# Attention scores on 32-row strips of TensorE, one strip for each head of a group of four, in place of a block-diagonal key matrix

## What is computed

```python
x = x + jnp.tanh(g_xattn[0]) * _L0_xattn_ref(_layernorm(x, axis=-1), ctx_1024, ctx_1024, mask_Bx1xS2_if1, ...)
x = x + jnp.tanh(g_ffn[0]) * _L0_ffn_ref(_layernorm(x, axis=-1), L0_ffn_W1, L0_ffn_b1, ...)
...
scores = jnp.einsum('bhqd,bhkd->bhqk', q, k) / math.sqrt(hd)
scores = jnp.where(m == 0, NEG_INF, scores)
p_attn = jax.nn.softmax(scores, axis=-1)
```

## Time and profile before

| what | us |
|---|---|
| median of three runs | 288.04 |
| the profiled execution | 287.01 |
| its span, first to last instruction | 285.2 |
| outside the span | 1.8 |

### The profile page before, as it was taken

One profiled execution on the slowest core, in us unless ns is written; L12 is line 12 of the kernel. 1 busy time (PEld: TensorE's weight loads), 2 busy tenths in 40 slices (PEclk: granted clock), 3 DMA queues, 4 the chain that ended last, 5 costly groups with the idle time before them and its releaser, 6 DMA issues.

```text
span 285.2 us, 11006 instructions
## 1 busy us (share of the span) xinstructions
PE 229.3 (80%) x3785; PEld 193.4 (68%) x3785; DVE 189.1 (66%) x639; ACT 164.9 (58%) x482; POOL 180.3 (63%) x222
## 2 busy tenths in 40 slices
PE   1357888987988987789879896598789899999950
PEld 1245677765866765667768675376689799999950
DVE  4546778788798888988867868886575344444310
ACT  1236669696677886568865886436464344444410
POOL 5366757568467889467896686704877654555550
PEclk9999999999799999979996999979999999999995
DMA  7801466546543673314351221333143443110100
GB/s 216 230 15 28 102 148 169 143 103 144 144 129 79 171 177 67 105 32 126 67 150 37 42 48 34 76 85 86 45 143 91 123 119 79 50 33 24 39 21 0
DMA packets 58537, 26.53 MB, mean 93 GB/s; under 512 B 38608, under 2 KB 53989, under 8 KB 58484
## 3 DMA queue, kind: packets, MB, share of 16 engines
q1 hardware_dynamic: 55204, 20.02, 29.3%
q0 software_dynamic: 2272, 4.46, 4.7%
q10 hardware_dynamic: 1008, 1.35, 1.6%
HBM read 16.57 MB, written 5.51 MB: 77 GB/s over the span
## 4 chain that ended last, share of the span: by engine, by line
PE 43%; DVE 19%; issue 11%; ACT 10%; POOL 5%; DMA 5%; SPq 3%; DVEq 0%; POOLq 0%
PE ps L752 13%; DVE mx L1240 5%; PE ps L771 4%; PE ps L795 4%; PE ps L770 3%; PE ps L733 3%; PE ps L735 3%; PE ps L734 3%; ACT vx L644 2%; DVE qk L1185 2%; SPq L411 2%; ACT kT L630 2%; DMA w_r<-in_W_last_row 2%; ACT qk L616 2%; DMA kbd<-kT 2%
## 5 line engine op out<-in xcount | busy, mean ns | idle before, releaser
L565 POOL DMA_INDIRECT out<-fin,got x39 | 37.9, 971 | 28.2 <-DVE fin L1299 23.4
L1240 DVE TENSOR_REDUCE mx<-ps 128x16 f16<-128x1024 f32 x32 | 39.0, 1219 | 12.8 <-PE ps L813 12.7
L752 PE MATMUL ps<-w_f,hT 128*128 x312 | 44.6, 286 | 0.1
L517 POOL DMA_INDIRECT rows<-x_all,dest_i x32 | 33.3, 1041 | 17.0 <-DVE x_all L1075 9.5
L795 PE MATMUL ps<-vx,pr 128*64 128x32 f32 x1024 | 38.0, 229 | 4.9 <-DVE on L1175 4.0
L795 PEld LDWEIGHTS ps<-vx,pr 128*64 128x64 f32 x1024 | 34.5, 144 | 8.9 <-issue 5.3
L544 POOL TENSOR_TENSOR rot<-qk,cf 128x256 f32<-128x256 f32 x32 | 23.4, 732 | 24.7 <-ACT qk L616 17.6
L752 PEld LDWEIGHTS ps<-w_f,hT 128*128 128x128 f32 x312 | 37.8, 191 | 1.1 <-issue 0.3
L1299 DVE SCALAR_TENSOR_TENSOR fin<-ps,got 128x128 f32<-128x128 f32 x39 | 13.7, 351 | 35.9 <-PE ps L752 35.9
L531 POOL TENSOR_TENSOR stk<-rot,stk 128x256 f16<-128x256 f32 x32 | 21.5, 671 | 20.4 <-DVE stk L1253 20.4
L594 ACT ACTIVATE pr<-ps 128x1024 f32<-128x1024 f32 x32 | 32.7, 1021 | 2.2 <-PE ps L843 1.6
(11 more groups left out here) (158 smaller groups left out, 585.1 us busy)
## 6 DMA issues: line engine op xcount, KB each, us to landing
kbd<-kT SPq DMA_DIRECT2D x128, 32.0 KB, 2.5
got<-rows SPq DMA_DIRECT2D x39, 72.0 KB, 2.0
w_f<-in_W_rows SPq DMA_DIRECT2D x8, 256.0 KB, 2.9
w_r<-in_W_last_row SPq DMA_DIRECT2D x8, 256.0 KB, 3.2
w_f<-in_L_ffn_W SPq DMA_DIRECT2D x8, 256.0 KB, 4.7
x_all<-in_x SPq DMA_DIRECT2D x3, 512.0 KB, 5.2
xt_all<-in_x_t SPq DMA_DIRECT2D x3, 512.0 KB, 4.8
ct_all<-in_ctx SPq DMA_DIRECT2D x3, 512.0 KB, 4.5
```

What stands on the lines that cost most here:

```text
L517: pool.indirect_dma_start(out=rows, out_offset=bass.IndirectOffsetOnAxis(ap=dest_i[:, t:t + 1], axis=0), in_=x_all[:, t, :], in_offset=Non ...
L565: pool.indirect_dma_start(out=out_d, out_offset=bass.IndirectOffsetOnAxis(ap=got_i[:, u % GOT, R_ID:R_ID + 1], axis=0), in_=fin[:, u % FRI ...
L752: mm = pe.matmul(o, hT[:, par, c, :], w2_f[:, bass.ds(e, 1), c, :].rearrange("p o n -> p (o n)"), start=False, stop=(c == FC - 1))
L1240: dve.tensor_reduce(mx[:, t % 2, :].rearrange("p (w h) -> p w h", w=2)[:, :, 0:8], ps_s[:, :].rearrange("p (w h k) -> p w h k", w=2, k=S), ...
```

## The change

`kbd`, its zeroing (L488 on POOL, L886 on DVE), its four semaphores and its 128 transfers go. `kT` becomes a ring of four tiles, and ACT waits ahead of L630 for the transposed scores of four tiles earlier where it waited for `kbd` transfers. The score products contract one 32-row strip: 32 products of 64 columns for a tile, in two halves of 16, the first at the old place, the second behind the transpose L825, with a wait for the first half's completion. The transposed scores take 16 selector products and 32 others, each on one strip and 64 output rows. DVE's maximum reads the same 1024 columns and writes 4 by 4 values where it wrote 2 by 8. SP sends its later loads without the step loop.

```diff
+            def scores(t, half):
+                s = t % RING
+                for a in range(NA):
+                    for b in range(2):
+                        for w in (half, half + 2):
+                            r, c = head_rows(w), (NA * w + a) * S
+                            mm = pe.matmul(ps_s[S * b:S * b + S, c:c + S], qT[r, s, a, S * b:S * b + S],
+                                           kT[r, s, a, S * b:S * b + S], start=True, stop=True)
+                return mm
...
-                    pe.wait_ge(kbd_ld[s], (t // RING) * 64 + 64)
+                    pe.wait_ge(kT_ev, t + 1)
                     pe.wait_ge(qT_ev, t + 1)
                     wait(pe, mx_done, t)
-                    for a in range(NA):
...
-                    mm.then_inc(s_done, 1)
+                    scores(t, 0).then_inc(half_done, 1)
...
                     pe.transpose(ps_onT, on[:, t % 2, :], ident).then_inc(onT_done, 1)
+                t = i - 2
+                if live(t):
+                    pe.wait_ge(half_done, t + 1)
+                    scores(t, 1).then_inc(s_done, 1)
...
                     for a in range(NA):
-                        for w in range(2):
-                            r, c = rows_half(w), (NA * w + a) * P
-                            pe.matmul(ps_st[:, c:c + P], sel_h[r, a, :], mxT[r, par, :], start=True, stop=False)
+                        for w in range(4):
+                            r, c, k = head_rows(w), (NA * (w // 2) + a) * P, S * (w % 2)
+                            pe.matmul(ps_st[k:k + S, c:c + P], sel_h[r, a, :], mxT[r, par, :], start=True, stop=False)
                         for b in range(2):
-                            for w in range(2):
...
+                            for w in range(4):
+                                r, c, k = head_rows(w), (NA * (w // 2) + a) * P + S * b, S * (w % 2)
+                                mm = pe.matmul(ps_st[k:k + S, c:c + S], kT[r, s, a, S * b:S * b + S],
                                                qT[r, s, a, S * b:S * b + S], start=False, stop=(b == 1))
```

More of the change, by code:

```diff
@@ L81, in constants @@
         e[32 + i, i, :] = 1
-    sel = h[:, K_SEL:K_SEL + NA * P].reshape(P, NA, P)
-    for w in range(2):
+    sel = h[:, K_SEL:K_SEL + NA * S].reshape(P, NA, S)
+    for w in range(4):
         for a in range(NA):
-            for hh in range(2):
-                sel[64 * w + 2 * a + hh, a, S * hh:S * hh + S] = -1
+            sel[STK * w + a, a, :] = -1
     h[:, K_BASE:K_BASE + NE] = (CAP // P) * np.arange(NE)[None, :]
@@ L177, in build @@
         stk = sb("stk", [P, 2, WIN], F16)
-        kT = sb("kT", [P, 2, NA, P], F16)
+        kT = sb("kT", [P, RING, NA, P], F16)
         qT = sb("qT", [P, RING, NA, P], F16)
-        kbd = sb("kbd", [P, RING, 2 * NA, 2, S], F16)
         vx = sb("vx", [P, RING, 2, 8, 32])
@@ L396, in context_of @@
                 sp.dma_start(ct_all[:, a:b, :], ct_d[:, a:b, :]).then_inc(s_xt[c], 16)
[L398 to L432, removed]
@@ L434, in _, with expert_of @@
-            pipeline(step)
+            def expert_of(e):
+                wait(sp, s_w1lo, e - 1)
+                alone(sp, sp_passed)
+                sp.dma_start(w1_f[:, e % 2, :], W1[e, :, :]).then_inc(s_w1ld[e % 2], 16)
+                sp.dma_start(w1_r[:, e % 2, :], W1r[e, :, :]).then_inc(s_w1ld[e % 2], 16)
+                sp.dma_start(w2_f[:, e, :, :], W2[e, :, :].rearrange("(c p) d -> p c d", p=P)).then_inc(s_w2ld, 16)
+            columns_of(2)
+            context_of(2)
+            sp.dma_start(ids[:, :], const_i).then_inc(s_ids, 16)
@@ L437, in row_tile @@
+            expert_of(0)
+            columns_of(3)
+            context_of(3)
+            rows_of(3)
+            expert_of(1)
+            columns_of(4)
+            context_of(4)
+            rows_of(4)
+            sp.wait_ge(s_zb, 1)
+            alone(sp, sp_passed)
+            for r in (0, 32):
+                sp.dma_start(b2_f[r:r + NE, :], b2).then_inc(s_bld, 16)
+            for e in range(2, NE):
+                expert_of(e)
             def row_tile(t, slot, offset):
@@ L487, in _ @@
             pool.memset(vx[:, :, :, :, :], 0.0).then_inc(s_vz, 1)
-            pool.memset(kbd[:, 0:2, :, :, :], 0.0).then_inc(s_kz, 1)
             pool.wait_ge(s_cf, 16)
@@ L885, in _ @@
             dve.memset(mx[:, :, :], 0.0).then_inc(s_z1, 1)
-            dve.memset(kbd[:, 2:RING, :, :, :], 0.0).then_inc(s_kz2, 1)
             dve.wait_ge(s_z1, 5)
```

37 lines of the change are left out of this document (12 added, 25 removed).

## The result

| | before | after |
|---|---|---|
| median of four runs, us | 288.08 (286.25 to 291.29) | 294.4 (294.07 to 295.4) |
| the profiled execution, us | 287.01 | 294.33 |
| its span, us | 285.2 | 292.5 |
| mean granted clock | 0.958 | 0.942 |
| DMA packets; of these under 512 bytes | 58537; 38608 | 23729; 3792 |

The changed kernel is slower: the ratio of the runs is 1.0247, with a 95% interval from 1.0191 to 1.0303, so it lies about on the line of 2%. Three fifths of the transfers' packets went and the time rose by 6.3 us.

What follows compares the result with a forecast made beforehand. Two loops of nearly one length bound the attention steps, 4.54 us through the maximum and 4.81 through ACT. 6.9 + 3.6 + 1.4 + 0.6 - 3.3 = +9.2, plus 287.0 and 1.0, gives 297 us; range 285 to 306.

Steps and rivals of the forecast that it cites:

- the loop through the maximum: Ordinary attention step's loop from one DVE maximum through TensorE to the next: 4.53 us before, 5.14 forecast.
- The price of the halves: Score products in two halves around the transpose: 0.61 us more from first product to maximum, 1.08 in place of 0.47.
- the lower bound: Least added by the two halves: 0.41 us, starts packed twice as close because 64 columns stream in place of 128.
- the other signs named: Profile signs: L1240 larger in chain, halves some 0.6 us apart, DVE's score wait above 12.7, no `kbd` or expert-weight waits.
- The loop through ScalarE: Ordinary step's chain through ACT's row of copies and back to TensorE's projections, 4.81 us, a second loop.
- The lower ends of its terms: Least cost of 16 maximum-waiting steps (3.5), half-clock steps (2.4), 9 other steps (0.5), first three tiles (0.3), less 3.3 gains.
- The gains of 3.3 us: Waits that go: TensorE for `kbd` 2.8 us, DVE for expert weights 0.5; lesser bound 1.0 if next waits remain.
- The transposed scores at nothing: 48 products take 0.48 us side by side or 0.96, costed at nothing since the maximum covers them.
- Rival 1: Halves' added time under 0.27 us stays inside the slack of ACT's loop: 285 us, chance 0.13.
- Rival 2: Key transfers set more than their waits name; removing them speeds steps and half-clock stretches: 280 us, chance 0.12.
- Rival 3: 32-row strips don't run side by side, so the loop grows by 1.0 us: 309 us, chance 0.1.
- Rival 4: TensorE idles some 0.4 us more a step, bringing five more half-clock stretches, +8.5: 306 us, chance 0.1.

Runs made afterwards that it cites:

- run 1: `halves_together`: changed kernel with the second half of the score products directly behind the first, ahead of the transpose; 293.45 us, ratio 1.0105 to the kernel before.
- run 5: `transpose_first`: kernel before with the attention output's transpose moved ahead of its 64-row score products; 292.19 us, ratio 1.0137.
- run 9: `around_loads`: changed kernel with the score halves around the value products and later loads at the old steps; 291.48 us, ratio 1.0124 to the kernel before.
- run 10: `around_loads_x2first`: run 9 with VectorE's addition of the attention output ahead of its eviction of the queries; 293.62 us, ratio 1.0101 to the kernel before.
- run 3: `loads_in_steps`: changed kernel with later loads sent at the steps where the kernel before sent them; 297.17 us, ratio 1.02 to the kernel before.
- run 6: `st_strips_only`: kernel before with only the transposed scores' key products on 32-row strips, selectors still on 64 rows; 298.91 us, ratio 1.0352.
- run 2: `halves_around`: changed kernel with the first score half ahead of the value products, the second directly behind them; 295.99 us.
- early_loads_only: Kernel before, key matrix and transfers kept, with its later loads sent early; 296.28 us, ratio 1.0231.
- before_qkv_first: Kernel before with the next tile's projection products ahead of the maximum's transpose; 290.62 us, ratio 1.0146.
- before_x2first: Kernel before with VectorE's addition of the attention output ahead of its eviction of the queries; 287.61 us, ratio 0.9979.
- after_qkv_first: Changed kernel with the next tile's projection products ahead of the maximum's transpose; 307.01 us, ratio 1.0579 to the kernel before.
- st_strips_early: Kernel before with 32-row strips for the transposed scores' key products in the first 27 tiles alone; 297.62 us, ratio 1.0336.

## Why the prediction was right, and where its sum was not

The median of 294.4 lies 2.6 under the 297.0 forecast, and the direction came out for the reason given: the second half behind the transpose lengthens the loop through the maximum, which then sets the ordinary steps.

- **The price of the halves is the step that was mis-sized.** I took the upper bound, 0.61, on the ground that a half has as many products and loads as 16 products of before and would last as long. It measured 0.88 - 0.47 = 0.41, the lower bound to the hundredth: the 16 products of a half start within 0.13 us, where 16 of before needed some 0.2. That is not the half that the lower bound was worked out from, so the hundredth is luck. Steps are 4.95 and not 5.0 to 5.2, and the way to the maximum 0.88 and not 1.1; the other signs named came. The estimate by the Trainium skill's rule for loads ("TensorE: Matmul & The Clock Gate", section "LDWEIGHTS (loading the stationary operand)") spoke for the upper bound, four groups of four at 53 ns; the row speaks against it.
- **The loop through the maximum held.** 4.53 plus what lies newly between the value products and the maximum gives 4.94 for the change, 4.83 for run 1, 4.79 for run 5 and 4.69 for runs 9 and 10; measured are 4.95, 4.84, 4.79 and 4.69. **The loop through ScalarE did not**: its 4.81 is no floor, since before itself has a step of 4.51 and 4.76 as the mean of the 13. It was the length of one step, and its copies wait for VectorE's eviction (L596 for L1172, 42.4 us in all), which waits for TensorE's projection (L1172 for L765, 11.9 us in 25 tiles).
- **The sum.** The lower ends of its terms give 3.5 + 2.4 + 0.5 + 0.3 - 3.3 = +3.4. Steps 0 to 30 measured 166.46 - 162.29 = +4.2. The 13 short steps lost 0.23 each, where the forecast's own lower bound was 0.22 in a step that waited for scores and less in others.
- **The gains of 3.3 us came at most in part.** The six steps in which TensorE had waited for `kbd` (2, 3, 7, 8, 15 and 18) took 30.57 us and take 30.45. Set against the 0.23 that other steps lost, that is some 1.5 of the 2.8: a wait that went left the next one standing, as the lesser bound of that term has it.
- **What else makes up the 7.3 us** was not in the sum: a later first x (1.37, not the change's); TensorE's stops, 3.7 us in four, of which step 16 shows some 0.7 (5.79 against 5.09 in run 3); and 1.8 us from step 31 on, where a stop of 1.36 and the long half clock lie, whose shares aren't separated. The prediction had no term for the 1280 products more as instructions to be fetched. So 297 came near with one term too large, one gain too large and three terms missing, and that they nearly cancel is luck.
- **The transposed scores at nothing** held: 48 strips take as long as 24 products did. It held because the change moved the selectors to strips as well; run 6 shows the other case, 1.4 us.
- **Rival 1** (inside the slack) failed by its stated point, 0.41 against 0.27. **Rival 2** (the transfers gate more than their waits) failed: with the waits for `kbd` gone, the six steps that had them gained 0.12 us. **Rival 3** (strips don't run side by side) failed by a wide margin, 0.13 against the 0.4 for a half. The Trainium skill's 25 ns between starts ("TensorE: Matmul & The Clock Gate", section "Wait — 56ns, not 53.3ns?") fails with it: these starts lie some 8 ns apart. **Rival 4** (more half clock) came in part: 10.2 us more of it. Its reason, longer idle times in a step, is not what the profiles show: run 5 has steps of 4.8 and 17.1 us of half clock, run 2 has steps of 4.7 and 44.4.

## What to carry to other kernels

When an operation leaves the critical resource, look at what its order now puts between producer and consumer: here three fifths of the DMA packets went, the transfers had held TensorE for 2.8 us in all, and 0.41 us more in the loop of every step cost more. Price a block of small TensorE products by the start of its first and last one and by every change of tile size around it, not by the products' number. Count the products all the same: the seven kernels with 5065 of them stopped for 1.8 to 6.7 us in their profiles, which I read as waits for their instructions. Loads sent early are free only if nothing urgent stands behind them in the same queue.

## What the runs showed of the hardware that I had not expected

- **A change of tile size costs TensorE some 0.15 us** (run 6): 0.16 between the starts where 64-row selectors and 32-row strips alternate, while strips of one size begin 0.13 us for 16. The changed kernel has two more such changes in its loop, strips to the 128-row transpose and back; of the 0.25 from its first half to the transpose the starts of the half take 0.13.
- **Kernels with products on 32 rows ran longer at the lower clock around the start of the expert layer.** In one profile each, the length of the stretch that lies between 180 and 224 us: before 3.4, `early_loads_only` 3.4 twice, `transpose_first` 6.8, `before_qkv_first` 3.4, `before_x2first` 3.4 (and another 3.4 from 177.4 on); after 13.7, `halves_around`, `loads_in_steps`, `around_loads`, `around_loads_x2first` and `st_strips_only` 23.9 each, `halves_together` and `after_qkv_first` 27.3, `st_strips_early` 10.2. The means over all executions go the same way, but by little: beside the kernel before on the same chip the mean granted clock is lower by 0.004 to 0.025 in each of the eight kernels of the experiments that have such products, and higher by 0.004 to 0.014 in each of the four that have none. Single executions overlap (before has one at 0.910, `around_loads` one at 0.960). The stretch and the 5 us ahead of it, in before and in `loads_in_steps` (columns as in the earlier trace rows):

```profile
181.10:186.10 5.00, 3.29 (x93) 2.68 (x93) 3.79 (x13) 1.53 (x4) 4.11 (x4) 1.00 0.33 80
186.10:189.50 3.40, 3.40 (x66) 2.85 (x64) 2.54 (x8) 0.57 (x2) 0.00 (x0) 0.50 0.39 99
```

```profile
183.90:188.90 5.00, 3.07 (x117) 2.49 (x117) 3.79 (x11) 3.46 (x12) 2.94 (x5) 1.00 0.05 18
188.90:212.80 23.90, 21.47 (x398) 18.33 (x398) 13.71 (x56) 8.84 (x21) 8.96 (x9) 0.50 0.23 65
```

In the second (`loads_in_steps`) TensorE is busy 21.5 of 23.9 us at the granted clock 0.50, so it does not idle through the stretch. In both the fall follows 5 us in which TensorE worked less than on the mean of the attention steps (120.03 of 139.50 us, or 4.3 of 5): 3.29 us of them in before and 3.07 in `loads_in_steps`. Why the stretch is longer with strips is open.

- **TensorE can stop for 0.3 to 1.5 us with nothing to wait for.** All seven kernels with 5065 products do so in their profiles, 2 to 9 times, in steps 12 to 18 and 29 to 31 (waits ahead of the stacks' transposes left out); none of those with 3785 to 4297 does so behind a packet. Each of these 36 stops ends 1.2 to 1.6 us after the landing of a 16 KB packet of the instruction queue, which carries 43 of them in the seven kernels, 36 or 37 in the two with some 4200 and 33 in the others. That it is the fetch of TensorE's instructions is read from this; no run changed it alone.
